# A decoder layer on one core: the size of each expert matrix from its product with itself, and a step order written anew

## What is computed

```python
x = _layernorm(x + attn(x, Wq, bq, Wk, bk, Wv, bv, Wo, bo))     # 16 heads of 16, causal, top 32 scores kept
x = _layernorm(x + xattn(x, ctx_512, itok, proj_in, proj_out))  # 8 experts, hidden 512
x = _layernorm(x + ffn(x, weight))                              # Hadamard, 4-bit activations, ternary weights

# xattn
h = relu(einsum('edi,bsi->bsed', proj_in, x))
o = einsum('eid,bsed->bsei', proj_out, h)
gate = einsum('bks,bkse->bse', weights, one_hot(ensembles, E))
return einsum('bsei,bse->bsi', o, gate)
```

## Time and profile before

| | |
|---|---|
| median of 3 runs | 561.37 us (561.35 to 562.34) |
| profiled execution, its own time | 563.42 us |
| its span, first to last instruction | 561.6 us |
| busy: TensorE / weight loads | 517.0 (92%) / 444.1 |
| busy: VectorE | 463.3 (82%) |
| busy: ScalarE | 408.0 (73%) |
| busy: GpSimd | 346.3 (62%) |
| TensorE's mean granted clock | 0.962 of full |

### The profile page before, as it was taken

The page is one execution under the profiler, slowest core; times in us unless marked ns, Lnnn a source line. Parts: engine busy times, 40 slices in busy tenths (PEclk is TensorE's granted clock), DMA queues, the critical chain, the costliest instruction groups (busy, mean ns, idle before and its releaser), DMA issues.

```text
span 561.6 us, 22317 instructions
## 1 busy us (share of the span) xinstructions
PE 517.0 (92%) x8116; PEld 444.1 (79%) x8116; DVE 463.3 (82%) x2846; ACT 408.0 (73%) x1018; POOL 346.3 (62%) x355
## 2 busy tenths in 40 slices
PE   6566778999999999999899999999999999989973
PEld 5455567888888888888788888888888898878961
DVE  5999988897899899999998999998999995231325
ACT  3778988975948676877856887878787686656551
POOL 2557648865666466565546657657665748658581
PEclk9677989999999999999999999999999999999995
DMA  6853344010000100000100100100001000000001
GB/s 207 228 162 119 115 122 127 4 38 23 21 21 2 43 23 2 23 21 23 41 22 20 42 22 3 40 23 22 3 22 41 2 2 21 3 1 20 2 1 37
DMA packets 23773, 24.08 MB, mean 43 GB/s; under 512 B 2160, under 2 KB 20592, under 8 KB 23664
## 3 DMA queue, kind: packets, MB, share of 16 engines
q1 hardware_dynamic: 23664, 22.65, 13.7%
HBM read 18.32 MB, written 2.10 MB: 36 GB/s over the span
## 4 chain that ended last, share of the span: by engine, by line
PE 75%; POOL 3%; DVE 2%; issue 2%; ACT 1%; POOLq 0%; DVEq 0%; ACTq 0%
PE ps_z L945 29%; PE ps_o L961 28%; PE ps_misc L829 4%; PE ps_s L882 3%; PE ps_misc L919 3%; PE ps_pt L904 3%; PE ps_misc L837 2%; PE ps_misc L812 2%; POOL acc L617 1%; POOL h_lo L596 1%; POOL rstd L635 1%; DVE stats L998 0%; PE ps_s L891 0%; ACT x L650 0%; POOL var_eps L629 0%
## 5 line engine op out<-in xcount | busy, mean ns | idle before, releaser
L596 POOL TENSOR_TENSOR h_lo<-h_raw,h_hi 128x512 f16<-128x512 f32 x128 | 148.1, 1165 | 95.7 <-ACT h_raw L754 95.0
L961 PE MATMUL ps_o<-w_hi,h_lo 128*128 128x256 f16 x512 | 139.6, 273 | 0.3 <-POOL h_lo L596 0.3
L945 PE MATMUL ps_z<-x1t_hi,w_lo 128*128 128x256 f16 x512 | 139.8, 273 | 0.0
L945 PE MATMUL ps_z<-x1t_hi,w_hi 128*128 128x256 f16 x512 | 139.6, 273 | 0.0
L945 PE MATMUL ps_z<-x1t_lo,w_hi 128*128 128x256 f16 x512 | 139.6, 273 | 0.0
L961 PE MATMUL ps_o<-w_hi,h_hi 128*128 128x256 f16 x512 | 139.6, 273 | 0.0
L961 PE MATMUL ps_o<-w_lo,h_hi 128*128 128x256 f16 x512 | 139.5, 273 | 0.0
L750 ACT ACTIVATE h_hi<-ps_z 128x512 f16<-128x512 f32 x128 | 76.4, 597 | 60.7 <-PE ps_z L945 37.9
L1053 DVE MATCH_REPLACE8 taken<-next,taken 128x64 f32<-128x64 f32 (+4 forms) x480 | 110.5, 241 | 0.0
L617 POOL TENSOR_TENSOR acc<-go_sb,acc 128x512 f32<-128x512 f32 x55 | 70.0, 1272 | 35.7 <-ACT go_sb L764 34.7
L1048 DVE MAX8 next<-taken 128x8 f32<-128x64 f32 (+4 forms) x480 | 85.4, 243 | 0.2 <-issue 0.2
(11 more groups left out here) (149 smaller groups left out, 1025.3 us busy)
## 6 DMA issues: line engine op xcount, KB each, us to landing
w_raw<-in_w1t SPq DMA_DIRECT2D x8, 512.0 KB, 4.7
w_raw<-in_w2t SPq DMA_DIRECT2D x8, 512.0 KB, 5.7
v_pad<-v_sb SPq DMA_DIRECT2D x16, 136.0 KB, 3.1
xt_sb<-in_xt SPq DMA_DIRECT2D x8, 256.0 KB, 3.0
x_sb<-in_x SPq DMA_DIRECT2D x8, 256.0 KB, 2.8
xa_sb<-in_xt SPq DMA_DIRECT2D x7, 256.0 KB, 3.2
out<-out_sb SPq DMA_DIRECT2D x7, 256.0 KB, 2.2
ctx_sb<-in_ctx_w SPq DMA_DIRECT2D x8, 128.0 KB, 2.2
```

Of the source, the lines that this page charges most:

```text
L596: nc.gpsimd.tensor_tensor(h_lo[:, e % 2, 2 * z:2 * z + 2, :], h_raw[:, z, :, :], h_hi[:, e % 2, 2 * z:2 * z + 2, :], ALU.subtract)\
L945: last = pe.matmul(ps_z[z][:, d * UT:(d + 1) * UT], w[:, e, c, at:at + P], x[:, c, :], start=n == 0, stop=n == len(terms) - 1)
L961: last = pe.matmul(ps_o[e % 2][:, b * D:(b + 1) * D], h[:, e % 2, c, b * SEQ:(b + 1) * SEQ], w[:, e, c, :], start=n == 0, stop=n == len(te ...
```

## The change

`w1_squares` and `w2_squares` go. In their place a step `w_gram` on TensorE multiplies each matrix with itself: the matrix is cut into 8 blocks of 128x128, and the products of each block's transpose with the block are summed in PSUM, 16 products for the two matrices of an expert. The blocks are read as bf16 out of the fp32 tile, every second element, which is the upper half of each number. Then `w_abs` on ScalarE sums the absolute values of the two 128x128 results along each partition, and `w_sum` and `w_scale` go on as before, with 16 more in the divisor. The result only sets the power of two. `ps_o[1]` holds the product, so `ffn_sum` moves to `ps_z[1]`, and L1 of unit 0 waits for `ffn_prep`. `w_gram` of expert e waits for `w_abs` of expert e-1 and for both loads.

```diff
@@ -45,6 +45,7 @@
 STAGED = 2
 RING = 6
 EXPONENT = 1 << 23
+SPREAD = 16
 
 
 def keys(j):
@@ -112,7 +113,7 @@
     ("pool", "rstd3"), ("act", "ln3_apply"), ("sp", "store"),
 )
 AHEAD_STEPS = (("sp", "load_xa"), ("pe", "k"), ("act", "copy_k"), ("pe", "v"), ("act", "copy_v"))
-PREP_STEPS = (("sp", "load_w"), ("act", "w1_squares"), ("act", "w2_squares"), ("pe", "w_sum"), ("dve", "w_scale"),
+PREP_STEPS = (("sp", "load_w"), ("pe", "w_gram"), ("act", "w_abs"), ("pe", "w_sum"), ("dve", "w_scale"),
               ("act", "w1_high"), ("act", "w2_high"),
               ("pool", "w1_low"), ("pool", "w2_low"))
 
...
@@ -768,13 +767,12 @@
                     act.wait_ge(s_ffnw, 32)
                     act.activation(tmp_a[:, :, :], ffn_sb[:, :, :], ACT.Abs).then_inc(ffn_abs, 1)
                     act.activation(had_h[:, :, :], had_sb[:, :, :], ACT.Copy).then_inc(had_cast, 1)
-                elif name in ("w1_squares", "w2_squares"):
+                elif name == "w_abs":
                     e, = args
-                    i, raw, hi, loaded = ((0, w1_raw, w1_hi, w1_loaded) if name == "w1_squares" else
-                                          (1, w2_raw, w2_hi, w2_loaded))
-                    act.wait_ge(loaded[e % STAGED], 16 * (e // STAGED + 1))
-                    act.activation(hi[:, e, :, :], raw[:, e % STAGED, :, :], ACT.Square,
-                                   accum_out=w_sq[:, e, i:i + 1]).then_inc(w_squared[i], 1)
+                    act.wait_ge(w_gram_done, e + 1)
+                    act.activation(w1_hi[:, e, 0, 0:P], ps_o[1][:, 0:P], ACT.Abs, accum_out=w_sq[:, e, 0:1])
+                    act.activation(w2_hi[:, e, 0, 0:P], ps_o[1][:, P:2 * P], ACT.Abs, accum_out=w_sq[:, e, 1:2])\
+                        .then_inc(w_squared, 1)
                 elif name in ("w1_high", "w2_high"):
                     e, = args
@@ -860,7 +858,7 @@
                     pe.wait_ge(ffn_abs, 1)
                     pe.wait_ge(q_copied, GROUPS)
                     for c in range(CD):
-                        last = pe.matmul(ps_o[1][:, 0:D], ones[:, :], tmp_a[:, c, :], start=c == 0, stop=c == CD - 1)
+                        last = pe.matmul(ps_z[1][:, 0:D], ones[:, :], tmp_a[:, c, :], start=c == 0, stop=c == CD - 1)
                     last.then_inc(ffn_sum, 1)
                 elif name == "scores":
@@ -936,6 +934,7 @@
                         pe.wait_ge(x1t_low, v + 1)
                     if v == 0:
                         pe.wait_ge(w1_low_ready, e + 1)
+                        pe.wait_ge(ffn_prep, 1)
                     wait(pe, relu_done, 2 * i - 2)
                     for d in range(2):
@@ -962,12 +961,27 @@
                                          h[:, e % 2, c, b * SEQ:(b + 1) * SEQ], w[:, e, c, :],
                                          start=n == 0, stop=n == len(terms) - 1)
                     last.then_inc(l2_done, 1)
+                elif name == "w_gram":
+
+                    e, = args
+                    at = e % STAGED
+                    if e == 0:
+                        pe.wait_ge(q_copied, GROUPS)
+                    wait(pe, w_squared, e)
+                    for i, (raw, loaded, chunks, cols) in enumerate(((w1_raw, w1_loaded, CD, HIDDEN),
+                                                                     (w2_raw, w2_loaded, CH, D))):
+                        pe.wait_ge(loaded[at], 16 * (e // STAGED + 1))
+                        blocks = [(c, n) for c in range(chunks) for n in range(0, cols, P)]
+                        for n, (c, first) in enumerate(blocks):
+                            block = raw[:, at, c, first:first + P].bitcast(BF16)[:, 1::2]
+                            last = pe.matmul(ps_o[1][:, i * P:(i + 1) * P], block, block, start=n == 0,
+                                             stop=n == len(blocks) - 1)
+                    last.then_inc(w_gram_done, 1)
                 elif name == "w_sum":
                     e, = args
                     if e == 0:
                         pe.wait_ge(pool_const, 1)
-                    for i in range(2):
-                        pe.wait_ge(w_squared[i], e + 1)
+                    pe.wait_ge(w_squared, e + 1)
                     wait(pe, w_step, 3 * e - 2)
                     pe.matmul(ps_o[0][:, 0:2], ones[:, :], w_sq[:, e, :], start=True, stop=True)\
@@ -1113,7 +1127,7 @@
                 elif name == "ffn_ternary":
 
                     dve.wait_ge(ffn_sum, 1)
-                    V.tensor_scalar(wscale[:, :], ps_o[1][:, 0:D], 1.0 / D, 1e-5, ALU.mult, ALU.max)\
+                    V.tensor_scalar(wscale[:, :], ps_z[1][:, 0:D], 1.0 / D, 1e-5, ALU.mult, ALU.max)\
                         .then_inc(ffn_prep, 1)
                     dve.wait_ge(ffn_prep, 1)
@@ -1129,7 +1143,7 @@
 
                     e, = args
                     dve.wait_ge(w_summed, e + 1)
-                    V.tensor_scalar(w_ms[:, e, :], ps_o[0][:, 0:2], 1.0 / (HIDDEN * D), 1e-36, ALU.mult, ALU.max)\
+                    V.tensor_scalar(w_ms[:, e, :], ps_o[0][:, 0:2], 1.0 / (SPREAD * HIDDEN * D), 1e-36, ALU.mult, ALU.max)\
                         .then_inc(w_step, 1)
                     dve.wait_ge(w_step, 3 * e + 1)
```

More of the change, by code:

```diff
@@ L124 @@
     "pe": """
[L125 to L148, removed]
+        k q*2 k*2 scores v scores v ffn_sum w_gram w_sum turn_probs*2 q w_gram v w_sum scores k q scores
+        turn_probs w_gram w_sum turn_probs v turn_probs scores k w_gram w_sum k scores v attend turn_probs
@@ new lines @@
+        w_gram turn_probs attend turn_probs w_sum attend scores attend turn_probs turn_o out_proj turn_probs
+        w_gram v w_sum k turn_probs scores turn_x1 turn_probs w_gram v L1 attend L1 k L1 turn_probs w_sum L1*2
+        scores turn_probs q L1 w_gram attend w_sum scores attend turn_probs L2*4 L1 turn_probs L2*2 attend L1*2
+        scores L1*2 L2 turn_o turn_probs L1 out_proj L2*3 L1*2 L2 L1*2 turn_x1 scores L2 turn_probs v L1*2 L2*4
+        L1*2 L2 L1*2 L2 scores attend L1 turn_probs L2 turn_probs L1 turn_x2 L2*2 hadamard turn_probs L2
@@ new lines @@
+        L2 turn_probs L2 ffn L1*2 turn_probs L1 L2 scores L1*2 L2*2 L1 L2 L1 turn_x2 turn_probs L2 L1 scores L1
+        L2*2 attend L2 turn_probs attend L1 turn_probs attend L1*2 turn_probs hadamard L2 scores L2 attend L2*3
+        turn_o L1*2 out_proj L1*2 L2*2 scores turn_x1 L2 turn_probs L2 turn_q4 L1 ffn L1 turn_probs L1*2
+        turn_probs L1 L2*2 L1 L2 turn_probs L2 L1 turn_probs L2 attend L1*2 L2 L1 turn_probs L2*2 turn_probs
+        L1*2 attend L1 turn_x2 L2 turn_probs hadamard L2*2 attend L1 attend L1 turn_o L2 L1 out_proj L2*4
@@ L154 @@
[L154 to L162, removed]
-        ln2_stats gate_scale normalise first_max select*3 gate_sums*2 quantise select normalise keep select*2
@@ L174 @@
-        ffn_scale ln3_stats gated_last*2 ln2_stats*2 ln2_apply*2 x2t_low*2 quantise*2 ffn_scale ffn_residual
-        ln3_stats ffn_scale ffn_residual ln3_stats ln3_apply*2
+        gate_sums*2 first_max select first_max select*6 keep ffn_ternary select*3 w_scale select*4 w_scale
+        first_max keep select*5 first_max select*2 w_scale keep select*7 first_max keep w_scale select*4
+        first_max select normalise select*2 normalise keep w_scale normalise select normalise select*2 first_max
@@ new lines @@
+        gate_sums first_max x2t_low gate_sums normalise select*2 normalise select normalise select*3 keep
+        quantise select first_max normalise select*6 ln1_stats keep select*4 first_max x1t_low select*2
+        gate_scale ln2_stats gate_sums*2 ffn_scale select keep ln3_stats ln2_apply select*7 keep normalise*2
+        x2t_low quantise normalise*2 ln1_stats x1t_low gate_scale ln2_stats ffn_scale ln3_stats ln2_apply
+        x2t_low quantise ffn_scale ln3_stats gated_last*2 ln2_stats*2 ln2_apply*2 x2t_low*2 quantise*2 ffn_scale
```

148 lines of the change are left out of this document (81 added, 67 removed).

## The result

The changed kernel takes 573.27 us (median of 4 runs, 570.17 to 574.46) against 561.86 for the kernel before (4 runs beside it, 561.35 to 562.68): the ratio on record is 1.0188, with a 95% interval of 1.0164 to 1.0212 (the quotient of the two medians is 1.0203). The forecast was 563.8.

What follows compares the result with a forecast made beforehand. VectorE was taken to bound the head, TensorE the body, a chain of small steps the tail; +1.5 (seam) and +0.9 (tail) on 563.42 gave 565.8, less 2.05 for the median: 563.8 us, range 557.5 to 569.

Steps and rivals of the forecast that it cites:

- the start of L1: End of the head: terms -0.5 - 2.2 + 2 + 1, so L1 of unit 0 starts at about 91 us again.
- 28.6 idle us ..., so in themselves they cost nothing.: TensorE ahead of first L1: idle time covers all grams but the last; 7 us if that cover were gone.
- The waits named: In the head: exp (0,1) waits for a later score copy, 1 to 3 us; turn_x1 for ln1_apply, 1 us allowed.
- the +2 of the sum: Head, at keep (0,1): its exponential comes late, a wait between 1 and 3 us, the middle taken.
- Rival (b): Clearly slower: half clock between 26 and 37 us delays keep (0,1) and keep (0,2); +7.2, 568.6 us; chance 0.15.
- The gram: w_gram on TensorE: 16 products spaced 0.055 us, 1.0 us each, eight are 8 us; its stride free by the skill.
- The other side of the seam: First L1 to turn_probs (1,3): reached at 110.3 us, 2.1 earlier, but 3.6 us more work left behind it: +1.5.
- the body: First to last L2 stretch: same steps, same 431.5 us with 3.7 of gaps, no term, 2 us allowed either way.
- The tail: After the last L2: late ffn of unit 6 makes gated_last start 1.0 us after it, not 0.04: +0.9.

Runs made afterwards that it cites:

- e8: e2 with both gate_sums of unit 0 moved out of the head on VectorE, the next load_ctx moved behind: 566.25 us (1.0082).
- e7: Changed kernel with one 1 MB expert load moved behind the v_pad copies and load_ctx issued first again on SyncE: 570.38 us (1.0154).
- e3: Changed kernel with two scores steps moved away from the attends, by one to three steps: 570.55 us (1.0148).
- e2: Old order of the kernel before on all engines, with the new arithmetic, w_gram put ahead of each w_sum: 563.17 us (1.0022).
- e11: Old order with w_gram to first L1, then new; normalise(1,0) earlier, two L2 before scores at 113 us, unit 6's turn_q4 and ffn earlier: 570.97 us.
- e6: Changed kernel with one product of eight per matrix left in w_gram: 571.27 us (1.0174).
- e12: e9 without its edit at the end, so turn_q4 and ffn of unit 6 stand as in the changed kernel: 569.0 us (1.0129).
- e9: Changed kernel with one load behind the v_pad copies, two L2 ahead of scores at 113 us, unit 6's turn_q4 and ffn earlier: 571.68 us (1.0179).

## Why the prediction was wrong

The direction was right, the size was not: the range ended at 569.0.

1. **The step that failed is "the start of L1".** It counted VectorE's steps, took VectorE for the bound of the head, added its terms up to +0.3 us, and so let L1 start at 91 again; it started at 98.5, 7.6 later. VectorE did the predicted work, but TensorE's side came late: attend(0,3) ended at 79.5 us, turn_o began 8 us later than before, then out_proj at half clock. I read this as a head in which the engines hold each other up in turn; e8 and e7, in which work and a wait were taken off VectorE and L1 came no earlier, fit it. Of the 7.6 us, 4.2 go with the stall at 75 us (e3 starts L1 at 94.3; one execution, good to about 1.5 us). The other 3.4 against the kernel before are, by the account, 8.2 more work and 0.5 more loss by the clock, less 5.3 of idle time, with the error of the estimate. Which of the moved steps keeps the clock lower than in e2 (10.6 against 7.9 us lost) stays open; none was tried alone. It also stays open why L1 is late in e11, where the old order stands in the head: the v ahead of it explains a part of the 5.2 us, not all.
2. **"28.6 idle us ..., so in themselves they cost nothing."** True of the old order (e2). In the new one idle time gave back only 1.2 us; yet e6, with 6.4 us of products less, starts L1 at the same time, so there too the products' work is not what holds L1. Idle time in a head is cover only if the new step stands where the gap is.
3. **The waits named** did not come: keep (0,1) started at 39.85 instead of 37.48, without a wait for an exponential. That exponential ended at 39.25, late as forecast (38.2 to 40.3), but VectorE was late itself; 1.6 us of that was the later itok, a move on SyncE that the sum had left out. By keep (1,0) the delay was gone (72.14 against 72.15), so that the +2 of the sum came true for a moment and counted for nothing. Rival (b) had the wrong place too, though its size was the nearest.
4. **The gram** was sized well: 1.08 us at full clock, six of eight times, and products 0.057 us apart (0.055 predicted; the q4 row has 0.056), so the stride cost nothing, and the 81 ns of the Trainium skill ("TensorE: Matmul & The Clock Gate", Back-to-back issue gap) are not seen here. At half clock one took 1.76, and one waited 1.7 us inside for its load of w2. An absolute value takes 0.27 us, not 0.35.
5. **The other side of the seam and the body** (+1.5 and "I see no term"): 2.8 us from first L1 to last L2. The count was near: 20.5 us to turn_probs (1,3), at 119.05, instead of 18 to 20, and 435.5 behind it, as forecast (435). Against the kernel before work is 0.4 less, idle time 1.5 and clock 1.7 more: the stall of 2.30 at 116.55 us and the 3.5 us at half clock right behind it. In e12 the stall is 0.41 and the half clock gone.
6. **The tail**: gated_last was to start 1.0 us behind the last L2 and did, 0.93, but not for the reason given, so the right size was luck. GpSimd and VectorE in the changed kernel, against the earlier trace rows:

```profile
549.42 2.26 POOL L595 TENSOR_TENSOR h_lo<-h_raw,h_hi 128x512 f16<-128x512 f32 x2 [3.84 <-ACT h_raw L753]
551.65 1.27 POOL L616 TENSOR_TENSOR acc<-go_sb,acc 128x512 f32<-128x512 f32 x1
552.88 1.27 POOL L622 TENSOR_TENSOR t<-rounded,x 128x512 f32<-128x512 f32 x1
554.10 1.26 POOL L616 TENSOR_TENSOR acc<-go_sb,acc 128x512 f32<-128x512 f32 x1
...
555.47 0.88 DVE L1165 SCALAR_TENSOR_TENSOR acc<-ps_o,gate,acc 128x256 f32<-128x256 f32 x2
```

The predicted cause was the late ffn of unit 6. In e9 that ffn ends 10 us ahead of the last L2 (550.48), and gated_last still starts 0.93 behind it:

```profile
539.57 0.60 PE L827 MATMUL ps_misc<-tern_sb,q4t 128*128 128x256 bf16 x4
...
545.36 2.27 POOL L595 TENSOR_TENSOR h_lo<-h_raw,h_hi 128x512 f16<-128x512 f32 x2 [3.98 <-ACT h_raw L753]
...
551.41 0.88 DVE L1165 SCALAR_TENSOR_TENSOR acc<-ps_o,gate,acc 128x256 f32<-128x256 f32 x2
```

What is late is the last pair of h_low, which waits for a relu. That relu waits 4.21 us for an L2, though its own L1 is done, because it writes where that L2 reads. Three adds queue behind it on GpSimd.
